# Helper calls moved within and between the half-steps of a software-pipelined local attention block

## The reference

```python
h = shift_tokens(x)                      # half of the features come from the row before
q, k, v = split(h @ Wqkv, 3)             # heads of 64
q, k = l2norm(q) * qs, l2norm(k) * ksc   # unit length, then a learned scale
q, k = rotary(q, k)                      # cos and sin parts
sim = einsum(q, look_back(k)) * 8        # own window and the one before, masked
x = softmax(sim) @ look_back(v) @ Wo + x
h = shift_tokens(x)
h = (h - mean(h)) / sqrt(var(h) + 1e-5) * g + b      # layer norm
a, gate = split(h @ W1 + b1, 2)          # 341 + 341 columns
x = a * gelu(gate) @ W2 + b2 + x
```

## Time and profile before

| | us |
|---|---|
| median of 3 runs | 5118.23 (5112.92 to 5119.16) |
| the profiled execution, its own time | 5112.92 |
| its span in the trace | 5110.7 |
| L0 block stage | from about 750 to about 3950 in the span |
| L1 block stage | from about 4300 to about 5090 |

### The profile page before, as it was taken

How to read it: one execution, slowest core, us unless ns; L and a number is a source line. 1 busy time by engine, 2 the same in 40 slices (tenths; PEclk the granted TensorE clock), 3 DMA queues, 4 the chain that set the end, 5 groups by cost and what they waited for, 6 DMA issues and landing times. The chain is left out here.

```text
span 5110.7 us, 219416 instructions
## 1 busy us (share of the span) xinstructions
PE 4546.9 (89%) x81616; PEld 3416.9 (67%) x81616; DVE 3921.3 (77%) x8190; ACT 3158.8 (62%) x6718; POOL 2757.1 (54%) x3917
## 2 busy tenths in 40 slices
PE   4568948999999999999999999999998677988896
PEld 3556736777777777777777777777776455666665
DVE  6974567888888888888888888888885756777775
ACT  2003526777777777777777777777776445766675
POOL 0013126666666666666666666666664335555552
PEclk7987979999999999999999999999999789999998
DMA  2000125555555554555555555555553004434442
GB/s 76 1 1 24 42 66 132 142 139 142 137 139 140 137 143 134 143 131 149 134 149 130 149 135 147 131 149 132 145 135 90 10 18 116 114 105 114 111 111 73
DMA packets 704922, 564.39 MB, mean 110 GB/s; under 512 B 223492, under 2 KB 629864, under 8 KB 704008
## 3 DMA queue, kind: packets, MB, share of 16 engines
q1 hardware_dynamic: 691080, 537.36, 39.7%
q10 hardware_dynamic: 13312, 22.02, 1.4%
HBM read 359.38 MB, written 200.02 MB: 109 GB/s over the span
## 5 line engine op out<-in xcount | busy, mean ns | idle before, releaser
L2155 POOL TENSOR_TENSOR L_qk<-L_cos_part,L_sin_part 128x512 f32<-128x512 f32 x896 | 1132.3, 1273 | 110.8 <-DVE L_sin_part L2031 107.2
L1815 ACT ACTIVATE L_squares<-L_ps_q 128x512 f32<-128x512 f32 x896 | 533.1, 595 | 807.3 <-PE L_ps_q L1541 800.6
L1541 PE MATMUL L_ps_q<-L_w_qkv,L_xT 128*128 128x512 f32 x1792 | 978.8, 629 | 22.7 <-DVE L_sin_part L2031 10.0
L2146 POOL TENSOR_TENSOR L_qk<-L_qk,L_rnorm 128x1024 f32<-128x1024 f32 (+1 forms) x512 | 864.1, 1688 | 18.2 <-POOL L_rnorm L2129 1.1
L1577 PEld LDWEIGHTS L_ps_t<-L_ident,L_qk 128*128 128x128 f32 x3584 | 446.6, 141 | 481.7 <-issue 381.8
L2030 DVE TENSOR_TENSOR L_cos_part<-L_ps_q,L_rot 128x512 f32<-128x512 f32 x896 | 610.5, 681 | 38.8 <-POOL L_rot L2165 30.6
L2031 DVE TENSOR_TENSOR L_sin_part<-L_ps_q,L_rot 128x512 f32<-128x512 f32 x896 | 610.0, 681 | 0.0
L2032 DVE TENSOR_REDUCE L_sumsq<-L_squares 128x8 f32<-128x512 f32 x896 | 605.7, 676 | 0.0
L2123 POOL TENSOR_TENSOR L_nw_a<-L_rnorm 128x32 f32<-128x32 f32 (+1 forms) x256 | 59.5, 232 | 1006.6 <-ACT L_rnorm L1845 1006.5
L1577 PE MATMUL L_ps_t<-L_ident,L_qk 128*128 128x128 f32 x3584 | 539.8, 273 | 8.2 <-DVE z L2095 4.4
L1826 ACT ACTIVATE L_qkT<-L_ps_t 128x512 f32<-128x512 f32 x896 | 531.2, 593 | 17.0 <-PE L_ps_t L1577 17.0
(11 more groups left out here) (293 smaller groups left out, 8966.3 us busy)
## 6 DMA issues: line engine op xcount, KB each, us to landing
L_val<-v_rows SPq DMA_DIRECT2D x896, 260.0 KB, 3.9
v_rows<-L_val SPq DMA_DIRECT2D x384, 260.0 KB, 2.2
v_rows<-L_val SPq DMA_DIRECT2D x512, 65.0 KB, 2.2
L_rot_base<-in_rot SPq DMA_DIRECT2D x256, 128.0 KB
v_rows<-L_val SPq DMA_DIRECT2D x128, 130.0 KB, 2.1
L_x_in<-x_rows SPq DMA_DIRECT2D x512, 32.0 KB, 1.7
mid_rows<-z SPq DMA_DIRECT2D x256, 64.0 KB, 1.6
L_f_in<-mid_rows SPq DMA_DIRECT2D x256, 64.0 KB, 2.0
```

Source lines behind the costliest of these rows:

```text
L1541: nc.tensor.matmul(ps_q[j % 2][:, :], xT[:, parity(t), :], w_qkv[:, 0:2, 256 * j:256 * j + 256], start=True, stop=True).then_inc(S["proj_p ...
L1815: nc.scalar.activation(squares[:, j % 2, :], ps_q[j % 2][:, :], ACT.Square).then_inc(S["sq_done"], 1)
L2146: nc.gpsimd.tensor_tensor(v, v, r, ALU.mult).then_inc(S["normed"], 1)
L2155: nc.gpsimd.tensor_tensor(qk[:, t % 2, h, s, :], cos_part[:, j % 2, :], sin_part[:, j % 2, :], ALU.add).then_inc(S["added"], 1)
```

## The change

Nothing is added or removed; helpers of three engines are called at another place, and in three of the four kinds of half-step `exponentials` and `prob_copy` change places.

- ScalarE, E0: `exponentials` is called ahead of the Gelu table load, where it came after the second table load. In L1 (`NS` = 1) `prob_copy` also goes ahead of the Gelu table load; in L0 it stays behind it. `deviation_roots` is called at the end of E0, behind `previous_keys`; it was in E1 behind `qk_copy`.
- ScalarE, E1, O0, O1: `exponentials` ahead of `prob_copy`. In E1 `normalised` is called ahead of both; it was last in the half-step.
- VectorE: `deviations` is called at the end of E0, behind `gated`; it was in E1 behind `normalise`.
- GpSimd, E1: `deviation_refine` is called ahead of `to_unit_length`; it was behind it.

```diff
@@ -1935,8 +1935,6 @@
                 def emit(k, T, hf):
                     square(k, T, hf, 0)
                     qk_copy(k, T, hf, 0)
-                    if hf == 1 and T % 2 == TO_LN % 2:
-                        deviation_roots(k, T)
                     out_copy(k, T, hf)
                     if hf == 0:
                         roots(k, T)
@@ -1944,24 +1942,29 @@
                         square(k, T, hf, 1)
                         qk_copy(k, T, hf, 1)
                     if hf == 0 and T % 2 == TO_UP % 2:
+                        exponentials(k, T, hf)
+                        if NS == 1:
+                            prob_copy(k, T, hf)
                         if live(k, T - TO_UP):
                             nc.scalar.preload_act_table_set("gelu_and_others")
-                        prob_copy(k, T, hf)
+                        if NS == 2:
+                            prob_copy(k, T, hf)
                         gates(k, T)
                         val_copy(k, T, hf)
                         if live(k, T - TO_UP):
                             nc.scalar.preload_act_table_set("natural_log_exp_and_others")
-                        exponentials(k, T, hf)
                     else:
                         val_copy(k, T, hf)
+                        if hf == 1 and T % 2 == TO_LN % 2:
+                            normalised(k, T)
+                        exponentials(k, T, hf)
                         prob_copy(k, T, hf)
-                        exponentials(k, T, hf)
                     if hf == 1:
                         input_copy(k, T)
-                        if T % 2 == TO_LN % 2:
-                            normalised(k, T)
                     else:
                         previous_keys(k, T)
+                        if T % 2 == TO_LN % 2:
+                            deviation_roots(k, T)
                         if T % 2 == TO_FT % 2:
                             affine(k, T)
@@ -2096,8 +2099,6 @@
                 def emit(k, T, hf):
                     normalise(k, T, hf)
-                    if hf == 1 and T % 2 == TO_LN % 2:
-                        deviations(k, T)
                     shift(k, T, hf)
                     for s in range(NS):
                         rotate(k, T, hf, s)
@@ -2106,6 +2107,7 @@
                         add_output(k, T)
                     elif T % 2 == TO_UP % 2:
                         gated(k, T)
+                        deviations(k, T)
                     else:
                         add_group(k, T)
@@ -2188,11 +2190,11 @@
                 def emit(k, T, hf):
                     if hf == 0:
                         refine(k, T)
+                    elif T % 2 == TO_LN % 2:
+                        deviation_refine(k, T)
                     if hf == 0:
                         mask_of_first_window(k, T)
                     to_unit_length(k, T, hf)
-                    if hf == 1 and T % 2 == TO_LN % 2:
-                        deviation_refine(k, T)
                     if hf == 1:
                         scaled_table(k, T)
```

## The result

The changed kernel takes 5227.3 us (median of 4 runs, 5225.7 to 5236.4) against 5116.9 before: ratio 1.022, 95% interval 1.0207 to 1.0232. The forecast was 5228. That the two agree to a microsecond is luck: two steps of L0's sum were wrong by 50 and 65 us with opposite signs, and L1's was some 15 us too dear. By the medians the change costs 110.4 us. The profiled execution's span is 5231.0, 120.3 over the one before, so this pair of executions lies 10 us further apart than the medians; the sum is taken apart in it.

What follows compares the result with a forecast made beforehand. TensorE's queue was taken to bound both block stages. 96 x 0.80 = 77 us in L0 plus 32 x 1.26 = 40 in L1, less some 2, added 115 to 5112.9: 5228 us, 8-in-10 range 5155 to 5268.

Steps and rivals of the forecast that it cites:

- What bounds it: Both block stages run at the pace of TensorE's queue, busy 98.6% in L0 and 89.7% in L1; only its stalls count.
- Groups times price: One group's loss or gain doesn't run into the next: 96 x 0.80 us in L0, 32 x 1.26 in L1.
- The exponential ahead of the load: E0: gates 0.52 us late in L0 and 0.79 in L1; TensorE's weighted values stall 0.41 and 0.79.
- `deviations` ahead of `normalise`: VectorE, L0: reciprocal and attention output 1.08 us late, so `out_transposes` is too, 0.41 of it already there.
- Given back: ... so the 0.29 stall at the output projection goes: E1 of L0: `deviations` no longer delays `shift`, so 0.29 us of 1.08 comes back, leaving 0.79.
- `out_transposes` on time: Sign in the profile after that the forecast is wrong: `out_transposes` in E1 doesn't wait for the late attention output.
- `prob_copy` behind `normalised` and the exponential, L0: E1: `prob_copy` ends at 2524.06, holding the scores from 2524.11 to 2524.13; the group's delay goes from 0.79 to 0.80 us.
- L1: E1's scores wait for `prob_copy` behind GpSimd's chain, `normalised` and the exponential: 1.26 us late in each of 32 groups.
- Costed at nothing: Moves taken to cost TensorE no time: the exponential and `prob_copy` exchange in O0 and O1, and `deviation_refine` ahead of `to_unit_length`.
- `deviation_refine` ahead of `to_unit_length`: GpSimd, E1: unit length is delayed by the root wait and a 1.85 us chain; its next-half-step reader loses nothing.
- The exchange in O0 and O1: Exponential ahead of `prob_copy`: copy about 0.5 us later, covered by TensorE's projection; cost nothing, 26 us left to the range.
- The faster one (5063): Rival, chance 0.10: `out_transposes` has slack, `deviations` costs nothing, stalls of 0.29 (L0) and 0.69 (L1) go, 50 us less.

Runs made afterwards that it cites:

- a2_dev: Kernel before with only `deviations` and `deviation_roots` moved to the end of E0 and `deviation_refine` ahead of `to_unit_length`: 5062.8 us, ratio 0.9915.
- b1_after_copyfirst: Changed kernel with `prob_copy` in E1 again directly behind the value copy, then `normalised`, then the exponential: 5142.6 us, ratio 1.0059 to the kernel before.
- c1_after_waitlast: Changed kernel with TensorE's wait for `prob_copy` ahead of the scores put behind its other three waits: 5198.6 us, ratio 1.0170 to the kernel before.
- a3_swap: Kernel before with only the exponential put ahead of `prob_copy` in E1, O0 and O1: 5119.6 us, ratio 1.0019.
- b4_clamp_scalar: Kernel before with VectorE's clamp (L2041) as a `tensor_scalar` with a constant instead of a two-input `tensor_tensor`: 5108.9 us, ratio 0.9997.
- b3_dev_in_gap: As the kernel before with `deviations`, roots and refine moved, but `deviations` ahead of `gated` in E0: 5042.6 us, ratio 0.9864 to the kernel before.

## Why the prediction was right, and where it was not

**What bounds it: right.** TensorE's queue sets the time in both stages, and each difference traced above is a stall made or removed there. Groups times price held: the change costs 0.93 to 0.95 us in each of L0's groups (90.4 / 95 between its first and last), as the half-steps show (0.40 in E0 and 0.54 in E1).

**The exponential ahead of the load: right in mechanism and size.** Forecast 0.41 and 0.79 for each group, measured 0.40 and 0.79 in E0, and 64 us alone where 96 x 0.41 + 32 x 0.79 = 65. (The view of waits shows only 0.2 of L0's 0.40, 10.7 us over 52; the half-step's length shows it whole.) The load itself takes 1.28 and the gates start 1.29 behind its start in L1 (4643.17 to 4644.46), so the 2.66 us that the Trainium skill gives (ScalarE: Activation LUTs, What ACT_TABLE_LOAD costs) are not paid here.

**`deviations` ahead of `normalise`: wrong in sign.** The prediction charged 1.08 - 0.41 = 0.67 for the attention output and gave back 0.29, +0.38 for each group of L0. The stall was there but smaller (1.89 - 1.40 = 0.49; the overlap of VectorE's operations and a slack of 0.07 had been left out), and what came back was 0.63: the input transpose starts 6.74 us into E1 where it started at 6.88, with 0.49 in between. So -0.14, and alone -0.25 in L0 and -0.71 in L1 (a2_dev). The step that failed is "Given back: ... so the 0.29 stall at the output projection goes": 0.29 is the idle time of the matmul row, and by the lengths of E1 and O1 the loss was 0.66. The sign of being wrong that the prediction named for this step, `out_transposes` on time, didn't come.

**`prob_copy` behind `normalised` and the exponential, L0: wrong in size.** Charged 0.01, measured 0.69 (b1_after_copyfirst takes it away: 64.6 us, 0.68 for each of 95). The copy itself was no later than forecast: its end at 2524.06 was 7.40 us into an E1 that starts 0.41 late, measured is 7.09. Two things around it were off: TensorE is at the scores 6.94 us into E1, and the forecast's own sum had it at 7.46 because too little was given back and too much charged; and a late wait costs more than the 0.07 that was reckoned, 0.51, of which 0.30 is the waits queued behind it (c1_after_waitlast). So of the 0.69 only 0.15 is the copy's own lateness (7.09 against 6.94).

These two errors nearly cancel: 96 x (0.38 + 0.14) = 50 too much, 96 x 0.68 = 65 too little. L0 came out at 90 for 77. The sum also started from the profiled execution's 5112.9 rather than from the median of 5118.2. Two slips in its additions weigh little: 2514.68 + 0.5 + 0.52 is 2515.70 and not 2515.72, and 2524.13 - 2523.32 is 0.81 and not 0.80, 1 to 2 us in 96 groups.

**L1: right in mechanism, too dear by the choice of the row.** Forecast 1.26 for each group; the usual group goes from 25.20 to 26.26 us, 1.06, by the starts of the Gelu loads. The group of the earlier trace rows isn't the usual one: in 15 of 19 groups of the kernel before E1 takes 6.8 us and not 6.4, as the next project waits for the output's addition as well. So it does here, two groups later:

```profile
4574.23 1.10 PE L1541 MATMUL L_ps_q<-L_w_qkv,L_xT 128*128 128x512 f32 x2 [0.36 <-DVE z L2049]
```

The change took that wait away too, as does a2_dev. 31 x 1.06 is 33, and the stage grew by 24.5; the rest lies at the sequences' starts and in the tail, where single groups gained up to 1.8 and lost up to 3.1; these are not taken apart.

**Costed at nothing.** `deviation_refine` ahead of `to_unit_length`: no wait of TensorE for `qk` beyond a few. The exchange in O0 and O1: 10 us by a3_swap's times, unexplained.

**The rivals.** The faster one (5063) had the right mechanism for its part: `deviations` at its new place is a gain, and alone it gives 5062.8. But not as it was put: it assumed that `out_transposes` would not stall, and it did, by 0.37; what paid was that the old loss was 0.66 and not 0.29. That its number is met is chance. It was outweighed by the other two moves, each of which puts a long operation ahead of one that TensorE is about to wait for.

## What to carry to other kernels

In a software pipeline find two rounds in which the bounding engine has the same instructions and compare their lengths: the difference is the loss, and here it was twice what the engine's own "idle" row said. Price a move from several groups, not from one. On an in-order queue put last the operation that nobody waits for soon, and among the waits of one instruction put last the one that is fulfilled last. A small piece of work belongs into an idle gap of its own engine, split if the gap is too short; on VectorE look also at what GpSimd runs at that time.

## What the runs showed of the hardware

- With three more waits on register values behind the one that came last, 0.51 us passed from the producer's end to the weight load (the changed kernel); with that one last, 0.21 (c1_after_waitlast). At `out_transposes`, where the late wait is the last one, it is 0.11 in the changed kernel (2501.70 + 0.69 to 2502.50). What makes up the 0.10 between the last two isn't shown; ahead of the scores TensorE's queue also raises a semaphore behind its waits.
- VectorE's small operations on SBUF take 0.16 to 0.2 us alone and up to 0.7 (two numbers for each partition) or 1.3 (the clamp) at some places of the list, whether they have one tensor input or two. The traces show what they end with. In the kernel before, all 121 clamps between 1500 and 3500 us start while GpSimd's addition (L2155) runs, and 119 of them end 0.045 to 0.06 us behind its end, whether it had 0.2 or 1.2 us left:

```profile
2522.89 1.27 POOL L2155 TENSOR_TENSOR L_qk<-L_cos_part,L_sin_part 128x512 f32<-128x512 f32 x1 [0.21 <-DVE L_sin_part L2031]
...
2523.53 0.68 DVE L2041 TENSOR_TENSOR L_nw_x<-L_sumsq,L_tiny 128x32 f32<-128x32 f32 x1
```

  So do 120 of 121 clamps of the one-input form (b4_clamp_scalar) and all 61 small additions of b3_dev_in_gap, which end 0.014 to 0.023 us behind it. In the changed kernel no long GpSimd instruction runs when that addition starts, and it takes 0.16 us 59 times out of 59. The Trainium skill (GPSIMD Engine Reference, Specifications) has GpSimd share its SBUF interfaces with VectorE and names contention with two-input operations and with those in a two-port mode, which the runs fit. A kernel with GpSimd's work taken away was not tried.
- ACT_TABLE_LOAD took 1.283 us all 260 times in each trace. Of the 256 loads in the block stages, 245 (before) and 248 (after) had the next activation 0.02 us or less behind their end.
